# Relation rows: four PSUM banks for the pair products, two for the tile products, two turns per loop branch

## What is computed

```python
h_proj = jnp.einsum('nd,rde->rne', h, relation_weight)
t_r = h_proj[etype, src]
h_r = h_proj[etype, dst]
att = jnp.sum(t_r * jnp.tanh(h_r + efeat), axis=-1)
...
a = att_exp / denom[dst]
msg = h[src] * a[:, None]
h_nb = jax.ops.segment_sum(msg, dst, num_segments=N)
```

## Time and profile before

| | |
|---|---|
| median of three runs | 8165.79 us (8153.4 to 8166.29) |
| the profiled execution | 8135.08 us, its span 8133.5 us |
| busy over the span | PE 48%, DVE 66%, ACT 28%, POOL 43% |
| pair products L715 | 3136 records of 423 ns, 715.8 us busy |
| sums L790 | 1568 of 281 ns, 440.2 us busy |
| one-hots of the tiles L567 | 57 of 6821 ns, 388.8 us busy |
| idle time of PE before L715 | 263.1 us, of it 178.3 put down to DVE's L790 |

### The profile page before, as it was taken

One profiled execution on the slowest core, in us unless ns is written; L12 is line 12 of the kernel. 1 busy time (PEld: TensorE's weight loads), 2 busy tenths in 40 slices (PEclk: granted clock), 3 DMA queues, 4 the chain that ended last, 5 costly groups with the idle time before them and its releaser, 6 DMA issues. The chain is left out here.

```text
span 8133.5 us, 102622 instructions
## 1 busy us (share of the span) xinstructions
PE 3894.0 (48%) x24731; PEld 3130.5 (38%) x24802; DVE 5407.7 (66%) x9588; ACT 2288.6 (28%) x3006; POOL 3503.5 (43%) x3810
## 2 busy tenths in 40 slices
PE   5777774000488826665362222223776222222476
PEld 2777773000388825565330000002763000001375
DVE  6777776968211146667437888885874888887686
ACT  5555553127122226566311111110001111111000
POOL 4766662001100067777515666661001666665100
PEclk9555555555699967877655555556975555555796
DMA  8899898955488723333336666663634666665462
GB/s 312 253 270 274 266 273 240 246 222 202 96 290 290 275 92 114 122 134 134 67 91 189 189 189 188 188 186 79 125 90 136 188 189 188 189 188 144 107 126 58
DMA packets 1551059, 1463.90 MB, mean 180 GB/s; under 512 B 1295757, under 2 KB 1343529, under 8 KB 1534460
## 3 DMA queue, kind: packets, MB, share of 16 engines
q1 hardware_dynamic: 976448, 824.48, 32.6%
q0 software_dynamic: 175712, 462.09, 20.9%
q10 hardware_dynamic: 398812, 176.37, 8.0%
HBM read 1080.92 MB, written 381.40 MB: 180 GB/s over the span
## 5 line engine op out<-in xcount | busy, mean ns | idle before, releaser
L2320 POOL DMA_INDIRECT rows_p<-node_rows,stage_i x1728 | 1638.0, 948 | 596.9 <-issue 482.7
L2356 PE MATMUL psZ<-parts_r,hot_t 126*128 x1728 | 629.6, 468 | 1859.8 <-DVE lz L2423 1720.0
L2356 PEld LDWEIGHTS psZ<-parts_r,hot_t 126*128 126x128 bf16 x1728 | 180.5, 104 | 2309.8 <-issue 2289.2
L2416 DVE TENSOR_TENSOR psZ<-psZ,rows_p 128x660 f32<-128x660 f32 x864 | 725.4, 847 | 476.1 <-DMA rows_p<-node_rows,stage_i 404.7
L257 POOL DMA_INDIRECT rows_s<-hpx,stage_i x784 | 740.5, 945 | 264.7 <-issue 240.7
L257 POOL DMA_INDIRECT both<-table,stage_i x784 | 740.5, 944 | 263.9 <-issue 239.7
L715 PE MATMUL psP<-window,pair_hot 128*128 x3136 | 715.8, 423 | 263.1 <-DVE pair_run L790 178.3
L715 PEld LDWEIGHTS psP<-window,pair_hot 128*128 128x128 f32 x3136 | 686.6, 331 | 295.8 <-issue 295.8
L2385 ACT ACTIVATE near<-locs,third 126x1536 bf16<-126x1536 bf16 x144 | 226.8, 1575 | 1923.4 <-DMA locs<-loc_rows 1923.3
L2423 DVE SCALAR_TENSOR_TENSOR lz<-psZ,att 128x660 f32<-128x660 f32 x864 | 722.9, 837 | 2.5
L2429 DVE TENSOR_REDUCE sc<-lz 128x10 f32<-128x660 f32 x864 | 711.8, 831 | 0.0
(11 more groups left out here) (523 smaller groups left out, 7527.7 us busy)
## 6 DMA issues: line engine op xcount, KB each, us to landing
tile<-adj SPq DMA_DIRECT2D x228, 781.2 KB, 4.6
xs<-x_src SPq DMA_DIRECT2D x648, 128.0 KB
x_src<-rows_p SPq DMA_DIRECT2D x144, 384.0 KB, 3.6
locs<-loc_rows SPq DMA_DIRECT2D x144, 378.0 KB
hpx<-stage ACTq DMA_DIRECT2D x25, 2048.0 KB, 7.5
pair_loc<-pair_locs SPq DMA_DIRECT2D x28, 1792.0 KB, 11.1
window<-hpx SPq DMA_DIRECT2D x196, 256.0 KB
dst_runs<-pair_run SPq DMA_DIRECT2D x28, 1792.0 KB
```

Of the source, the lines that this page charges most:

```text
L2320: pool.indirect_dma_start(rows[:, k, j, :], None, g.node_rows, bass.IndirectOffsetOnAxis(stage[:, k, j:j + 1], 0)).then_inc(got[k], 16)
L2356: last = pe.matmul(psZ[:, n % 4, j, 0:ZH], hot[:, k, col * CE:(col + 1) * CE], parts[:, bass.ds(at[col], 1), :].rearrange("p o c -> p (o c)"),
L2416: v.tensor_tensor(here, here, rows[:, k, m * G:(m + 1) * G, 0:ZH], ALU.add).then_inc(added, 1)
```

## The change

`psP` gets four banks and not two: PE may begin batch n when the sums of batch n - 4 are done, and the counts of `chained` that others wait for are shifted by as much (it now begins at 32 plus 1). `Tiles.RING` goes from 4 to 2, so `psA` has two banks. The bank of a batch must be a number at the time when the program is written, and a turn has 14 batches, no multiple of four; so PE's and DVE's loops run seven times over two turns each, written out one after the other, where they ran 14 times over one. The loops of SP, ACT and POOL stay as they are, and so do all transfers, products, sums and their sizes.

```diff
-    RING = 4
+    RING = 2
...
+    AHEAD = 4
...
-        psP = s.ps("psP", [P, 2, BP * D])
+        psP = s.ps("psP", [P, AHEAD, BP * D])
...
-                    sp.wait_ge(chained, x * PC + (PC + 17))
+                    sp.wait_ge(chained, x * PC + (PC + AHEAD * BP + 1))
...
-                with pe.Fori(0, NCH // 2) as i:
-                    for n in range(2 * M):
...
-                            last = pe.matmul(psP[:, n % 2, j * D:(j + 1) * D], hot[:, n % 2, j * CE:(j + 1) * CE],
...
+                with pe.Fori(0, NCH // 4) as two_turns:
+                    for u in range(2):
+                        i = two_turns * 2 + u
+                        for n in range(2 * M):
...
+                            pe.wait_ge(chained, batch(i, n) * BP + 9)
+                            for j in range(BP):
+                                last = pe.matmul(psP[:, (u * 2 * M + n) % AHEAD, j * D:(j + 1) * D], hot[:, n % 2, j * CE:(j + 1) * CE],
...
-                v.sem_inc(chained, 16)
+                v.sem_inc(chained, AHEAD * BP)
...
-                        v.wait_ge(chained, batch(i, n) * BP + (j + 17))
+                        v.wait_ge(chained, batch(i, n) * BP + (AHEAD * BP + 1 + j))
...
-                with v.Fori(0, NCH // 2) as i:
-                    c.begin(i, TB)
-                    c.turn = i * TB + before
-                    c.n = 0
...
+                with v.Fori(0, NCH // 4) as two_turns:
+                    c.begin(two_turns, 2 * TB)
+                    for u in range(2):
+                        i = two_turns * 2 + u
+                        c.turn = i * TB + before
+                        c.n = 0
...
```

More of the change, by code:

```diff
@@ new lines, in _ @@
+                with pe.Fori(0, NCH // 4) as two_turns:
+                    for u in range(2):
+                        i = two_turns * 2 + u
+                        for n in range(2 * M):
+                            k, m = divmod(n, M)
+                            rel = nc.values_load_multi_w_load_instructions(
+                                g.pair_rel[0:1, bass.ds(batch(i, n) * BP, BP)], engines=[mybir.EngineType.PE], min_val=0, max_val=BP - 1,
+                                skip_runtime_bounds_check_because="bounded where the table is made")[1]
+                            pe.wait_ge(window_in[n % 2], i * (16 * M) + (n // 2 + 1) * 16)
+                            pe.wait_ge(hot_ready, batch(i, n) + 1)
+                            pe.wait_ge(chained, batch(i, n) * BP + 9)
+                            for j in range(BP):
+                                last = pe.matmul(psP[:, (u * 2 * M + n) % AHEAD, j * D:(j + 1) * D], hot[:, n % 2, j * CE:(j + 1) * CE],
+                                                 window[:, n % 2, bass.ds(rel[j], 1), :].rearrange("p o c -> p (o c)"),
+                                                 start=True, stop=True)
+                            last.then_inc(paired, 1)
+                            for at in (2 * m, 2 * m + 1):
+                                r, part = 2 * k + at // Tiles.NG, at % Tiles.NG
+                                tiles.products(pe, i * TB + r, r, part, i * (TB // 2) + r // 2)
@@ L788, in runs @@
                         at = m * BP + j
-                        v.wait_ge(chained, batch(i, n) * BP + (j + 17))
+                        v.wait_ge(chained, batch(i, n) * BP + (AHEAD * BP + 1 + j))
                         v.scalar_tensor_tensor(run[:, k, at, :], run[:, k, at - 1, :] if at else run[:, 1 - k, PC - 1, :],
-                                               same[:, k, at:at + 1], psP[:, n % 2, j * D:(j + 1) * D], ALU.mult,
+                                               same[:, k, at:at + 1], psP[:, (u * 2 * M + n) % AHEAD, j * D:(j + 1) * D], ALU.mult,
                                                ALU.add).then_inc(chained, 1)
                 before = c.n
-                with v.Fori(0, NCH // 2) as i:
-                    c.begin(i, TB)
-                    c.turn = i * TB + before
-                    c.n = 0
[L799 to L807, removed]
+                with v.Fori(0, NCH // 4) as two_turns:
[4 more added lines that the diff above has]
+                        c.n = 0
+                        for n in range(2 * M):
+                            k, m = divmod(n, M)
+                            runs(i, n, u)
+                            if m == 1:
+                                tiles.one_hots(c, v, i * TB + (2 * k + 1), 1, i * (TB // 2) + k)
+                            if m == 5:
+                                tiles.one_hots(c, v, i * TB + (2 * k + 2), 0, i * (TB // 2) + (k + 1))
+                    c.n = before + 2 * TB
+                c.end(NCH // 4)
 def relation_scores(nc, g):
```

4 lines of the change are left out of this document (2 added, 2 removed).

## The result

The changed kernel takes 8175.5 us in the median of nine runs (8168.8 to 8188.7), the kernel before 8161.3 us in nine on the same chip (8151.7 to 8166.5). The ratio over all runs is 1.0023, with an interval of 1.0014 to 1.0032 (the medians alone are 0.18% apart): 0.23% slower, where I had forecast 0.1% faster and given "slower" 0.12. The time of 8175.5 us lies in the range, the sign is wrong.

The account below looks back on a forecast made before the run. In relation_rows each half turn was bound by a saturated DMA queue up to the m = 3 window, then PE's own four batches. Terms 0 + 0 - 8.4 + 0 = -8.4 us took 8165.8 to 8157.4 us; range 8139 to 8184.

Parts of the forecast that it names:

- The banks for `psP`: Pair products in relation_rows: four banks let PE run four batches ahead of DVE; taken as 0 us, at most 178.3 us.
- The reading behind it: Batch m = 3 of each half turn waits about 5 us for its window load, not for DVE as the profile says.
- The two banks for `psA`: Tile products in relation_rows: ample cover for the moves, so 0 us; last tile 0.8 us later as the bound.
- The removed returns: PE's loop head in relation_rows: seven of 13 returns go, each worth 1.2 us, 8.4 us saved in all.
- second rival: Half-turn boundaries: earlier m = 0 pulls in window and pair_loc loads, saving 28 x 0.9 = 25 us, 8140; chance 0.11.
- its own 1.2 us: Gain per removed PE return, taken between PE's own part of 1.03 us and the whole difference of 1.8 us.
- 39.7 us: Forecast length of half turns now beginning inside the doubled turn, at ACT's return; between today's two kinds, 39.2 and 40.9.
- The longer body: PE's and DVE's returns to a loop body of twice the length: taken to cost 0 us.
- The bound from above: Return to the longer body: at most a fetch behind the full DMA queue, 11.1 us at 6 returns, 67 us.
- the third rival: PE's or DVE's six returns stall to fetch the long body: 5.5 us each, 33 us less 8.4, 8190; chance 0.10.
- 4.1 us on PE: Stall per PE return from which the change would be over 0.2% slower: (16.3 + 8.4)/6.
- The prediction let the clock stay low: TensorE's clock in relation_rows: stays at 0.50, its lower level of 1.2 GHz, since nothing makes PE denser.

Follow-up runs that it names:

- `banks_only`: Kernel before with four banks for psP and two for psA, loops still over one turn: ratio 0.9996 to the kernel before.
- `late_locs`: Kernel before with the load of pair_loc issued after the window of m = 5 and not of m = 2: ratio 1.0035.
- `pe_short`: Kernel before with PE's loop over two turns and four 128-column pair products a batch for eight of 64, fixed window rows, results not the reference's: 8047.7 us.
- `pe_seven`: Kernel before with seven turns written out on PE, so that it returns once and not 13 times, banks as before: ratio 1.0004.
- `dve_two_banks`: Kernel before with DVE's loop alone over two turns, four banks for psP and two for psA: ratio 1.0014.
- `turns_only`: Kernel before with PE's and DVE's loops over two turns each, banks as before: ratio 1.0031.
- `pe_two`: Kernel before with PE's loop alone over two turns, banks as before: ratio 1.0030, on another slower chip 1.0014.
- `dve_two`: Kernel before with DVE's loop alone over two turns, banks as before: ratio 1.0030, on another slower chip 0.9994.
- `before_here`: The kernel before, unchanged, run again on a slower chip for its profile: 9475.7 us.

## Why the prediction was wrong

**The banks for `psP`** (0 us): right. `banks_only` measured 0.9996 on a slower chip, and in the changed kernel's own trace the wait at m = 3 put down to DVE was still there with four banks. The reading behind it, that m = 3 waits for its window, was right (`late_locs`, and the true name in the row at 380.97).

**The two banks for `psA`** (0 us, 0.8 in the tail): right. In the tail the products do wait for the moves now, and the last store is issued 4.6 us after the first product (1342.53 after 1337.92) where it was 4.0. It still lies behind `dst_runs`; the next stage starts 12.35 us after it and started 12.88 after it before:

```profile
1337.92 1.02 PE L585 MATMUL psA<-hot 128*128 128x125 bf16 x8 [4.88 <-DVE hot L567]
...
1339.28 1.08 PE L585 MATMUL psA<-hot 128*128 128x125 bf16 x8 [0.34 <-ACT tile L603]
...
1342.53 0.33 SPq L611 DMA_DIRECT2D adj<-tile  x1
...
1354.88 0.35 SPq L854 DMA_DIRECT2D ef<-in_ef  x1
```

**The removed returns** (-8.4 us): right in sign, too large. m = 0 came about 1 us earlier as I had it (1.37 us of idleness against 2.30), but the half turn became 0.5 us shorter, not 1.2. m = 1 started 7.6 us after the issue of `t_rows`, as before: ACT's and SP's returns, which stayed, hold it and with it the window of m = 3. The prediction says against its second rival that ACT holds m = 1, and did not apply that to its own 1.2 us. Such half turns were to take 39.7 us and took 40.3. Times six it is 2.9 us, and 3.4 for all seven.

**The longer body** (0 us): this is the step that failed. I had written: "I take nothing, for all 13 returns now show only 1 us." That is no evidence. A return to a body that is held says nothing about one that is not; the trace of before could only show that 859 records of PE and 265 of DVE are held. The bound from above that I kept, 11.1 us a return, was of the right kind, and the third rival had the mechanism, the place, and the point from which it decides, 4.1 us on PE. The measured 4.7 us, 4.5 more than before, lies just above that. (The 4.1 took each us at the return to be a us of the time; that is not so, as the next paragraph shows.) I gave it 0.10. The Trainium skill (Runtime: NRT & Kernel Launch, Instruction fetch mechanics) says that a taken branch out of what is held forces a fetch before execution goes on. The traces agree: instruction packets and a branch of 4.7 us come together, and go together in `pe_short`. By the rule's figures, 512 instructions on DVE and 2048 on PE, fetched in blocks of 256, 416 and 1716 records should have been held, and neither was, unless instructions without a record of their own, 96 and 332 of them, make up the rest. For PE `pe_seven` speaks against that: its 45 packets of 16 KB in 1600 us, at 126 us a turn there, are 3.5 a turn, an estimate of 7 packets for a body of two turns, where 2048 instructions in such blocks would be 8. For DVE no run shows it. The rule deserved most of the chance for at least DVE, and I gave its presence in the text no weight in the sum.

Of 4.5 us more per return 2.7 us reached the half turn (41.1 to 43.8). In the mean of the six, m = 0 started 4.1 us later than before, m = 1 and the issue of the window of m = 3 some 3 us later, and m = 3 itself 2.7 us later. At 6 returns that is 16.1 us. DVE's 34 us did not add to it: DVE was back at 368.58, `pair_run` of m = 0 and 1 was done by 374.2, and no batch from m = 1 on waited for it. Over the six, m = 3 started 11.2 us after its window was issued, 11.6 before. That is read from this trace; PE's loop or DVE's doubled alone was timed only on the other chips, where PE's cost something on both.

**What is left open.** The 12 half turns that begin in the middle of a turn, with neither kind of boundary, grew by 0.54 us each, 6.5 us. That the packets take DMA time from the windows is a guess, and the other chips are divided on it. On that of 9486 us such half turns were longer with packets (61.6 us before, 62.1 in the changed kernel, 62.2 in `pe_seven`, 62.5 in `dve_two_banks`). On that of 9351 us `turns_only` and `pe_two`, with packets, took 60.8 us like `banks_only` without, and `dve_two` 61.3.

## What to carry to other kernels

Writing out more turns of a loop is not free when the body stops being held: ask how long the loops are that the trace shows returning without a fetch, and give a body beyond the longest of them the price of a fetch at every return; either keep the body under it or write out so many turns that hardly a return is left. Where the profile names an engine for a wait, find when that engine was done; here the name was wrong at the place that mattered, and more buffers for it were worth nothing. And a gain at one engine's loop edge is shared with the engines whose edges stay.

## What was not expected of the hardware

- PE's return took 4.7 us at 1716 records of body and 0.2 us at 1016; DVE's 5.7 us (34.0 us in 6) at 528, 4.2 us at 416 and none at 265. In such records DVE's limit lies between 265 and 416, PE's between 1016 and 1716.
- Reading straight on through a body of seven turns (`pe_seven`) cost nothing that its interval, 0.9990 to 1.0018, can show, with one 16 KB packet (0.74 MB in 45) every 36 us.
- Fewer and wider fp32 pair products: 1568 records of 128 columns at 404 ns in `pe_short` against 3136 of 64 columns at 423 ns. TensorE's granted clock was 0.62 in that stage in place of 0.50, with PE busy 49% of the time in place of 76%: it went to and fro between its two levels. The 1208 records that began at the lower one took 438 ns in the mean, so twice the columns cost 15 ns more there; the 360 at the higher one took 287 ns. The prediction let the clock stay low because nothing makes PE denser; here it rose where PE was less busy. Here are the rows of `pe_short`:

```profile
196.00:1204.00 1008.00, 495.97 (x2968) 436.23 (x2968) 824.79 (x1700) 599.08 (x783) 742.36 (x808) 0.62 0.98 294
...
L717 PE MATMUL psP<-window,pair_hot 128*128 128x128 f32 x1568 | 362.1, 404 | 373.3 <-DMA window<-hpx 157.2 <-ACT pair_hot L742 128.1 <-DVE pair_run L792 87.7
```

- The same program took 8161 us on one chip and 9351 to 9498 us on others. In `before_here` this stage takes 638 of the 1341 us that its span is longer, with standstills of PE, DVE, ACT and SP at once; the rest lies in later stages and is unexplained.
